# Forward wave of a DTW alignment: halo shuffle issued before the minimum, the scan waits for both

## The reference, cut to what matters

```python
def _dtw_cost(D):
    row0 = jnp.cumsum(D[0])
    def row_step(prev_row, d_row):
        first = d_row[0] + prev_row[0]
        def col_step(left, inp):
            d_ij, up, diag = inp
            r = d_ij + jnp.minimum(jnp.minimum(up, left), diag)
            return (r, r)
        _, rest = lax.scan(col_step, first, (d_row[1:], prev_row[1:], prev_row[:-1]))
...
x = x + jnp.tanh(g_xattn[0]) * _L0_xattn_ref(ctx_1024, _layernorm(x, axis=-1))
```

## Time and profile before

| | |
|---|---|
| median of the runs | 866.72 us (866.27 to 867.23) |
| the profiled execution | 865.79 us |
| its span in the trace | 864.1 us |
| TensorE busy | 679.6 us, 79% of the span, 3115 matmuls |
| VectorE (DVE) busy | 646.6 us, 75%, 1829 instructions |
| ScalarE (ACT) busy | 412.3 us, 48% |
| GpSimd (POOL) busy | 414.4 us, 48% |
| chain that ended last | TensorE 69%, DVE 20%, issue 4%, DMA 3% |
| mean granted TensorE clock | 0.865 of full speed |

### The profile page before, as it was taken

One profiled execution on the slowest core, in us unless ns is written; L12 is line 12 of the kernel. 1 busy time (PEld: TensorE's weight loads), 2 busy tenths in 40 slices (PEclk: granted clock), 3 DMA queues, 4 the chain that ended last, 5 costly groups with the idle time before them and its releaser, 6 DMA issues.

```text
span 864.1 us, 12936 instructions
## 1 busy us (share of the span) xinstructions
PE 679.6 (79%) x3115; PEld 542.2 (63%) x3115; DVE 646.6 (75%) x1829; ACT 412.3 (48%) x757; POOL 414.4 (48%) x451
## 2 busy tenths in 40 slices
PE   4322310006899999999999978999998999999996
PEld 2211100006688888888888857999876888888884
DVE  6579856999777777777777777677786777777774
ACT  2434200004465565556556545454545556556563
POOL 5557720002466666666666643111025666665663
PEclk9755555555799999999999987999969999999999
DMA  5464571002386777767776700000046766666661
GB/s 122 75 129 134 139 114 13 0 0 52 71 179 139 154 147 142 158 138 160 140 154 144 155 1 9 2 0 0 1 97 125 162 143 152 146 143 157 137 158 50
DMA packets 84163, 89.44 MB, mean 104 GB/s; under 512 B 48957, under 2 KB 61858, under 8 KB 80608
## 3 DMA queue, kind: packets, MB, share of 16 engines
q1 hardware_dynamic: 79808, 79.38, 44.5%
q0 software_dynamic: 4320, 9.68, 3.9%
HBM read 79.84 MB, written 8.70 MB: 102 GB/s over the span
## 4 chain that ended last, share of the span: by engine, by line
PE 69%; DVE 20%; issue 4%; DMA 3%; ACT 2%; POOL 1%; SPq 1%; DVEq 0%; POOLq 0%; ACTq 0%
PE bank L1011 14%; PE bank L1012 13%; PE bank L1013 13%; DVE junk L1419 7%; PE bank L1147 6%; PE bank L1144 6%; PE bank L1145 6%; PE bank L1075 4%; PE bank L1057 2%; DVE arena L1376 2%; DVE arena L1385 1%; PE bank L947 1%; DVE arena L1384 1%; DMA arena<-scr_d 1%; DVE arena L1386 1%
## 5 line engine op out<-in xcount | busy, mean ns | idle before, releaser
L699 POOL TENSOR_TENSOR act_lo<-arena,act_hi 128x512 fp32r<-128x512 f32 x232 | 300.3, 1294 | 200.6 <-ACT act_hi L833 200.6
L1639 DVE TENSOR_TENSOR bank<-arena,bank 128x512 f32<-128x512 f32 x232 | 160.7, 693 | 105.9 <-PE bank L1013 73.5
L845 ACT ACTIVATE arena<-bank 128x512 f32<-128x512 f32 x232 | 138.9, 599 | 179.6 <-PE bank L1013 177.4
L1011 PE MATMUL bank<-xn_hi,w_hi 128*128 128x512 f32 x464 | 185.9, 401 | 3.0 <-DVE arena L1647 3.0
L1012 PE MATMUL bank<-xn_hi,w_lo 128*128 128x512 f32 x464 | 185.7, 400 | 0.0
L1013 PE MATMUL bank<-xn_lo,w_hi 128*128 128x512 f32 x464 | 185.0, 399 | 0.0
L1647 DVE TENSOR_TENSOR arena<-bank,arena 128x512 f32<-128x512 f32 x232 | 160.5, 692 | 19.8 <-DVE bank L1639 9.2
L833 ACT ACTIVATE act_hi<-arena 128x512 fp32r<-128x512 f32 x232 | 145.3, 626 | 12.8 <-DVE arena L1647 12.8
L1011 PEld LDWEIGHTS bank<-xn_hi,w_hi 128*128 128x128 f32 x464 | 88.3, 190 | 26.3 <-DVE arena L1647 4.3
L1013 PEld LDWEIGHTS bank<-xn_lo,w_hi 128*128 128x128 f32 x464 | 88.4, 191 | 21.2
L1012 PEld LDWEIGHTS bank<-xn_hi,w_lo 128*128 128x128 f32 x464 | 88.3, 190 | 20.8
(11 more groups left out here) (199 smaller groups left out, 963.1 us busy)
## 6 DMA issues: line engine op xcount, KB each, us to landing
arena<-scr_mask SPq DMA_DIRECT2D x94, 512.0 KB, 6.7
scr_w<-prep_out POOLq DMA_DIRECT2D x25, 192.0 KB, 2.2
w_raw<-scr_w SPq DMA_DIRECT2D x25, 192.0 KB, 6.5
arena<-scr_one SPq DMA_DIRECT2D x6, 512.0 KB, 5.8
w_raw<-in_L_ffn_expert_gate_k SPq DMA_DIRECT2D x32, 64.0 KB, 6.0
w_raw<-in_L_ffn_expert_up_k SPq DMA_DIRECT2D x32, 64.0 KB, 5.8
w_raw<-in_L_ffn_expert_down_k SPq DMA_DIRECT2D x64, 32.0 KB, 5.3
prep_in<-in_L_ffn_wg POOLq DMA_DIRECT2D x21, 64.0 KB, 2.4
```

The source lines that it names most:

```text
L699: nc.gpsimd.tensor_tensor(act_lo[:, k % 2, :], act_a[:, k % 2, :], act_hi[:, k % 2, :].bitcast(F32), ALU.subtract).then_inc(FF[f]["alo"], 1)
L845: nc.scalar.activation(act_s[:, k % 2, :], ps[4 + k % 2][:], ACT.Silu).then_inc(FF[f]["silu"], 1)
L1011: nc.tensor.matmul(out, w_h, x_h, start=start, stop=False)
L1639: nc.vector.tensor_tensor(ps[6 + i][:], act_s[:, i, :], ps[6 + i][:], ALU.mult).then_inc(FF[f]["t"], 1)
```

## The change

The shuffle is written ahead of the minimum. Since the shuffle no longer stands between the minimum and the scan, the minimum now counts up a new semaphore, `wave_upper`, and the scan waits for it in addition to `wave_halo`.

```diff
+        s_upper = sem("wave_upper")
...
                 prev, cur = rst[:, s, :], rst[:, s + 1, :]
                 if s >= MST:
                     dve.wait_ge(s_steps, s - MST + 1)
-                nc.vector.tensor_tensor(mst[:, s % MST, :], prev[:, 1:CW + 1], prev[:, 0:CW], ALU.min)
                 nc.vector.stream_shuffle(cur[:, 0:1], prev[:, CW:CW + 1], shift).then_inc(s_halo, 1)
+                nc.vector.tensor_tensor(mst[:, s % MST, :], prev[:, 1:CW + 1], prev[:, 0:CW], ALU.min).then_inc(s_upper, 1)
                 nc.vector.tensor_tensor(lg[:, s, 1, :], prev[:, 0:CW], prev[:, 1:CW + 1], ALU.is_le)
                 dve.wait_ge(s_halo, s + 1)
+                dve.wait_ge(s_upper, s + 1)
                 nc.vector.tensor_tensor_scan(cur[:, 1:CW + 1], mst[:, s % MST, :], dl[:, s, :], cur[:, 0:1],
                                              ALU.min, ALU.add).then_inc(s_scan, 1)
```

## The result

The changed kernel takes 870.27 us (median of 20 runs, 866.99 to 872.79), the kernel before in the same comparison 865.89 us (20 runs, 862.96 to 872.46): a ratio of 1.0039, 95% interval 1.0021 to 1.0057. It is slower by 0.39%, some 3.4 us by the ratio and 4.4 us by the medians. The sign is the one forecast, the size is short of the 5.8 us, and 870.27 us lies just under the range.

A forecast was written before the change was run, and what follows sets the result against it. The wave was taken as bound by DVE's dependent cycle with its waits, on the kernel's path. Period 0.625 to 0.688 us over 92 slots adds 5.8 us: 866.72 + 5.8 = 872.5 us, range 870.5 to 875.5.

The forecast's parts named there:

- What bounds the wave: DVE's cycle of minimum, shuffle and scan: both waits bind, not DVE's instruction rate; 0.625 us per slot before the change.
- The swap alone: Shuffle ahead of minimum in each slot, waits no dearer: scan starts 0.012 us earlier per slot, 1.1 us over 92 slots.
- The second wait: Scan's wait on the same slot's minimum becomes an EVENT_SEMAPHORE: scan 0.063 us later per slot, period 0.688, 5.8 us over 92.
- the lag behind it: From the minimum's end to the scan's start, through the EVENT_SEMAPHORE: taken as 0.11 us, between 0.09 and 0.13.
- the mask load: LOAD_MASK_SELECT ahead of the shuffle, now behind the wave_row wait: taken as 0, at most 14 ns, 1.3 us over the wave.
- The step that failed: Store and reload after the wave share DMA queues with weight turning until about 118 us; gain from a later wave taken as 0.
- So a microsecond more or less in the wave is a microsecond of the kernel: From the wave's start to the backward chase's end, only one line of dependent steps moves the end, so wave changes count fully.
- the sign that everything behind the wave would keep its length: Check in the later profile: all stretches after the wave keep their length and shift by the same amount.
- The first: Rival: the scan's new wait is no dearer than the old ones, only order counts; 865.6 to 866.4 us, chance 0.08.
- The second rival: After the late EVENT_SEMAPHORE DVE's instruction stream becomes the bound: period 0.75 us, 11.5 us more, 878.2 us; chance 0.07.
- The third: Rival: a true gain over 0.2%, needing the scan at 0.287 us or earlier in the slot; chance 0.03.

The follow-up runs named there:

- the second comparison: The changed kernel measured once more, unaltered, against the kernel before: 868.53 against 865.78 us, ratio 1.0031 (1.0006 to 1.0056).

## Why the prediction was right in kind and short in size

- **What bounds the wave.** Right. Both waits of the cycle bind, and in the kernels that change only order and waits the period followed from the later of shuffle and minimum plus the lag of its wait: 0.613 forecast and 0.6155 measured, 0.625 and 0.6275, 0.692 and 0.6928.
- **The swap alone.** Right: 0.012 us per slot forecast, 0.010 measured (0.6252 to 0.6155).
- **The second wait.** Right in mechanism, 0.688 forecast and 0.682 measured. Three terms were off and partly cancel: the minimum takes 184 ns instead of 194 (-0.010), the lag behind it is 0.105, nearly the 0.10 of L1644 and not 0.11 (-0.005), and the mask load, costed at 0, adds nearly 0.01, since the shuffle starts 0.045 after the scan's end (48.65 + 0.285 = 48.935, then 48.98) where the minimum had started after 0.035. Over the wave: 5.2 us instead of 5.8.
- **The step that failed** is this one: "if the wave ends 5.8 us later less of that is left, worth between 0 and a few tenths of gain; I take 0." It measured 1.8 us (31.5 to 29.7). With it fell "So a microsecond more or less in the wave is a microsecond of the kernel" and the sign that everything behind the wave would keep its length. The turning's end at 117.8 us was read as a fixed time, by which a store that begins 5 us later would still meet about half of it, and even that half was not priced. But 117.8 was itself a result of the collision: left alone, the turning ends near 113 us. When the wave ends at 110 the two meet for 3 us instead of 12, and 1.8 of the 3.3 us by which the stretch was longer beside the turning (31.5 against 28.2) are spared, 1.0 in store and reload and 0.8 in the last transfer, the latter by a way that is not shown. Single profiles scatter: the stretch is 30.9 to 31.5 us in the four with a short wave and 29.0 to 29.7 in the four whose last scan starts at 110 to 111 us, and the means of the two groups are again 1.8 us apart. 5.2 - 1.8 is 3.4 us, which is the measured ratio; that it fits so closely is luck, as the interval runs from 1.8 to 4.9 us and the second comparison gave 2.7.
- **The rivals.** The first, a wait that costs nothing, is what comes out when the waits are written in the other order; with the waits as the change has them it is excluded. The rule that I set against the trace, from the Trainium skill's "VectorE: DVE Perf Modes", section "The DRAIN you can't avoid", that a semaphore costs nothing extra, agrees with the order of before plus an early wait in the instruction stream, which cost 0.002 us per slot, and not with a late one there, which cost 0.07. What a wait that stays with its instruction costs against none at all, no run here shows. The second rival, an instruction stream that can't keep up, did not occur: it needed a period of 0.75 us. The third, a true gain over 0.2%, did not either; even with the late wait on the scan the period fell by only 0.010 us.
- **The range** was cut at 870.5 on the belief that the sum's unknowns lay in the lag. It should have gone down to what lies behind the wave as well. The median of before, 865.89 us in this comparison instead of 866.72, took a further 0.8 us off; three runs do not fix a median when single executions spread over 9 us. The other way, the medians of this comparison differ by 1.0 us more than the ratio says (4.4 against 3.4); the changed kernel's lies in the upper of its two groups of executions. So 872.5 - 0.6 - 1.8 - 0.8 + 1.0 = 870.3 us.

## What to carry to other kernels

When an instruction has two waits, write the one that is met last first, so that it stays with the instruction and the early one goes into the instruction stream; or let both producers count up one semaphore. In a chain of short dependent instructions this was worth 0.07 us each time, some six times the 0.012 that the reordering could gain. And the end time of background work in a profile is not a constant: if it shares the DMA engines with the path, moving the path moves it, so price the overlap by the stretch of the path with the background taken away.

## What the runs showed of the hardware that was not expected

- A wait in front of a `stream_shuffle` goes to its LOAD_MASK_SELECT, and the shuffle then starts 0.043 to 0.045 us after the awaited end, against 0.035 for a `tensor_tensor` in the same place.
- The 128x32 minimum takes 184 ns behind a shuffle and 194 ns behind L1376, 0.9 us over the wave; with the order of before it is 194 ns again, with a wait added or the turning held back, but 186 where an added comparison stands between L1376 and it. Whether the instruction in front or the late wait makes the difference was not tried.
- Plain small DVE instructions behind each other start about 0.10 us apart (48.37 to 48.47 for L1386 and L1387), closer than the 0.12 that the timeline of before shows for them, which was a wait in each case or the mask load.
- The low clock stretch of the attention comes in two lengths, 17.1 and 23.9 us, in executions of the same kernel. What decides between them stays open.
